# One tensor for the last stage's expert weights, lent to the first two stages, and the expert loads moved from SyncE at the last stage's start to ScalarE in and behind the last batch

## The reference: what is computed

```
x = x + tanh(g_xattn[0]) * L0_xattn(layernorm(x), ctx, mask0)      # 16 heads of 16
x = x + tanh(g_ffn[0])   * L0_ffn(layernorm(x))                    # 8 experts, top 2
x = x + tanh(g_xattn[1]) * L1_xattn(ctx, layernorm(x), mask1)      # 16 heads of 64, keys: 375 + 112
x = x + tanh(g_ffn[1])   * L1_ffn(layernorm(x))                    # 8 experts, top 2

def L1_ffn(x, W1, b1, W2, b2, Wr, br):       # W1: 8 x 256 x 1024, W2: 8 x 512 x 256
    logits = xf @ Wr + br
    topk_val, topk_idx = top_k(logits, 2); scores = softmax(topk_val)
    h = einsum('nd,edh->enh', xf, W1) + b1;  a, g = split(h, 2)
    out_e = einsum('enh,ehd->end', silu(a) * g, W2) + b2
    return sum of the two chosen experts' outputs, weighted by scores
```

## Time and profile before

| | |
|---|---|
| median of three runs | 1396.94 us (1396.32 to 1399.18) |
| the profiled execution | 1397.87 us, its span 1396.1 us |
| granted TensorE clock, mean | 0.944 of full speed |
| PE, VectorE, ScalarE, GpSimd busy | 88%, 77%, 71%, 58% of the span |
| first stage ends, last stage begins | about 449 us, 1186 us |
| DMA | 185.50 MB, mean 133 GB/s |

### The profile page before, as it was taken

The page is one execution under the profiler, slowest core; times in us unless marked ns, Lnnn a source line. Parts: engine busy times, 40 slices in busy tenths (PEclk is TensorE's granted clock), DMA queues, the critical chain, the costliest instruction groups (busy, mean ns, idle before and its releaser), DMA issues. The chain is left out here.

```text
span 1396.1 us, 38073 instructions
## 1 busy us (share of the span) xinstructions
PE 1224.2 (88%) x13060; PEld 878.1 (63%) x13060; DVE 1080.9 (77%) x3112; ACT 996.9 (71%) x2552; POOL 813.6 (58%) x1204
## 2 busy tenths in 40 slices
PE   5899999999985599999999999999999974489994
PEld 3677777777763245666656666656666653388994
DVE  4899999999984268888888888888888882477772
ACT  4888888888873368888787888787888771256662
POOL 3545445455423445777777777777777674146564
PEclk8899999999997699999999999999999985699998
DMA  6546455344310149777688877888777693853323
GB/s 185 149 135 176 121 158 165 110 136 144 105 51 21 42 97 164 152 141 152 140 158 163 157 141 149 139 159 162 157 136 153 139 197 58 323 150 57 61 36 76
DMA packets 309406, 185.50 MB, mean 133 GB/s; under 512 B 257930, under 2 KB 295186, under 8 KB 306112
## 3 DMA queue, kind: packets, MB, share of 16 engines
q1 hardware_dynamic: 293024, 140.82, 46.8%
q0 software_dynamic: 13168, 35.80, 10.4%
q10 hardware_dynamic: 3024, 6.47, 1.6%
HBM read 76.19 MB, written 49.94 MB: 90 GB/s over the span
## 5 line engine op out<-in xcount | busy, mean ns | idle before, releaser
L1685 ACT ACTIVATE b_prob<-b_prob,b_top 112x487 f32<-112x487 f32 x256 | 178.8, 698 | 28.6 <-DVE b_top L1811 26.9
L1318 POOL TENSOR_TENSOR b_halves<-b_prob,b_halves 112x487 f16<-112x487 f32 x128 | 146.8, 1147 | 80.6 <-ACT b_halves L1710 79.2
L1496 PE MATMUL b_ps_p<-w_s,b_tok_s 128*128 128x512 f16 (+1 forms) x768 | 187.7, 381 | 4.0 <-DVE b_k_s L1798 3.2
L1496 PE MATMUL b_ps_p<-b_tok_s,w_s 128*128 128x487 f16 x768 | 183.1, 376 | 6.4 <-POOL b_tok_s L1312 3.7
L1811 DVE CUSTOM_DVE_ANT_0 b_prob<-b_ps_s,b_keep 112x487 f32<-112x487 f32 x256 | 167.4, 655 | 13.6 <-PE b_ps_s L1589 12.0
L721 ACT ACTIVATE a_prob<-a_prob,a_top 112x375 f32<-112x375 f32 x256 | 155.0, 606 | 5.4 <-DVE a_top L856 2.3
L1710 ACT ACTIVATE b_halves<-b_prob 112x487 f16<-112x487 f32 x256 | 155.9, 609 | 0.4
L856 DVE CUSTOM_DVE_ANT_0 a_prob<-a_ps_s,a_keep 112x375 f32<-112x375 f32 x256 | 138.2, 540 | 14.8 <-PE a_ps_s L614 14.6
L622 PE MATMUL a_ps_t<-a_const,a_prob 112*125 112x112 f32 x768 | 134.2, 284 | 12.7 <-ACT a_prob L721 10.4
L861 DVE TENSOR_TENSOR a_pT<-a_ps_t,a_pT 125x336 f16<-125x336 f32 x256 | 128.2, 501 | 20.5 <-ACT a_pT L728 19.5
L1604 PEld LDWEIGHTS b_ps_o<-b_v_s,b_pT 128*128 128x128 f16 (+1 forms) x3072 | 123.7, 99 | 31.9 <-DMA b_pT<-b_halves 12.0
(11 more groups left out here) (263 smaller groups left out, 3016.8 us busy)
## 6 DMA issues: line engine op xcount, KB each, us to landing
xs<-a_blank SPq DMA_DIRECT2D x14, 1032.0 KB, 4.2
c_w_pool<-w_split SPq DMA_DIRECT2D x8, 1600.0 KB, 10.1
b_wch_f<-in_w_experts POOLq DMA_DIRECT2D x32, 384.0 KB, 5.1
w_split<-b_wch_s POOLq DMA_DIRECT2D x32, 384.0 KB, 3.4
a_k_stack<-keys SPq DMA_DIRECT2D x96, 93.8 KB, 3.2
a_ctx_f<-in_ctxT SPq DMA_DIRECT2D x16, 375.0 KB, 3.9
keys<-a_k_s SPq DMA_DIRECT2D x16, 375.0 KB, 3.2
b_ctx_t<-in_ctx SPq DMA_DIRECT2D x16, 375.0 KB
```

The lines of the kernel that those rows point to most:

```text
L1318: pool.tensor_tensor(halves[:, h % TURN, LO, 0:NK], prob[:, h % RING, 0:NK], halves[:, h % TURN, HI, 0:NK], ALU.subtract).then_inc(s_lo[1], 1)
L1496: last = pe.matmul(out, sta(a, k), mov(m, k), start=(k == 0 and n == 0), stop=(k == tiles - 1 and n == 2))
L1685: act.activation(prob[:, h % RING, 0:NK], prob[:, h % RING, 0:NK], ACT.Exp, bias=top[:, h % RING:h % RING + 1], scale=-1.0, accum_out=sums ...
```

## The change

`w_pool`, 128 x 8 x 6400 fp16, is allocated in `build_program` for the whole kernel, with the eight semaphores `s_w`. The first two stages take a part of their buffers out of it (`room` cuts pieces off one after another). In the second stage the first piece is `k_s` and `v_s` of even batches (15,984 of the 51,200 columns), so the places of experts 0 and 1 (columns 0 to 12,799) are free once batch 14's values are done; the other six lie over buffers that batch 15 still uses. ScalarE now issues all eight loads: experts 0 and 1 in slots 7 and 9 of batch 15, the other six behind the last batch, between `hitem` 1 and `hitem` 3 of the tail. SyncE's list in the last stage keeps the tile loads, with one `announce` behind each of the first eight.

```
+def room(tensor):
+
+    flat = tensor[:, :, :].rearrange("p e n -> p (e n)")
+    taken = [0]
+
+    def take(shape, dt):
+        n = math.prod(shape[1:]) * (2 if dt == F32 else 1)
+        part = flat[0:shape[0], taken[0]:taken[0] + n]
+        taken[0] += n
...
-        k_s = [sb(f"k_s{i}", [128, 2, IT, NK], F16) for i in range(2)]
-        v_s = [sb(f"v_s{i}", [128, 2, NB1, INNER], F16) for i in range(2)]
+
+        k_s, v_s = zip(*((take([128, 2, IT, NK], F16), take([128, 2, NB1, INNER], F16)) for i in range(2)))
...
-        halves = sb("halves", [T, TURN, 2, NB1 * KB1], F16)
-        pT = sb("pT", [128, TURN, 2, NB1, 128], F16)
+        halves = take([T, TURN, 2, NB1 * KB1], F16)
+        pT = take([128, TURN, 2, NB1, 128], F16)
+        tok_f = take([128, KT, NK], F32)
+        order = take([T, T], F32)
+        x2_n = take([T, D], F32)
...
+            def load_expert(e):
+
+                need(act, s_pv, H, B - 2 if e < 2 else B - 1, H)
+                if e >= 2:
+                    for j in range(2):
+                        act.wait_ge(s_wchstore[j], 16 * B)
+                act.dma_start(w_pool[:, e, :], w_dram[e]).then_inc(s_w[e], 16)
+
             def body(b, par):
                 for s in range(H):
+                    if not ahead(b, 1) and s in (7, 9):
+                        load_expert((s - 7) // 2)
...
             for k in range(HI_):
                 hitem(B - 1, k)
+                if k == H_O - 1:
+                    for e in range(2, E):
+                        load_expert(e)
             weigh(B - 1)
...
-            def load_expert(e):
-                sp.dma_start(w_pool[:, e, :], w_dram[e]).then_inc(s_w[e], 16)
-
-            load_expert(0)
             for i in range(TILES):
-                if i == 4:
-                    announce(0)
-                    load_expert(1)
-                elif i == 8:
-                    announce(1)
-                    load_expert(2)
-                    load_expert(3)
-                elif i == XT:
-                    for e in range(4, E):
-                        load_expert(e)
-                    announce(2)
-                if XT <= i < XT + E - AHEAD - 1:
-                    announce(i - XT + AHEAD + 1)
                 load(i)
+                if i < E:
+                    announce(i)
```

More of the change, by code:

```diff
@@ L12 @@
+import math
 from contextlib import ExitStack
@@ L63 @@
 BLANK = 128 * 8
+def room(tensor):
[5 more added lines that the diff above has]
+        taken[0] += n
+        part = part.bitcast(F32) if dt == F32 else part
+        axes = "abcde"[:len(shape) - 1]
+        sizes = dict(zip(axes[1:], shape[2:]))
+        return part.rearrange("p (" + " ".join(axes) + ") -> p " + " ".join(axes), **sizes) if len(axes) > 1 else part
+    return take
 def need(eng, sem, per, batch, count, met=None):
@@ L109, in phase_attention_small_heads @@
         sem = lambda name: ctx.enter_context(nc.semaphore("a_" + name))
+        take = room(w_pool)
         bank = lambda name: ctx.enter_context(nc.psum_tensor("a_" + name, [128, 512], F32))
@@ L121, in phase_attention_small_heads @@
         WE = E * D // (H // 2)
-        next_f = sb("next_f", [128, next_w_dram.shape[1]], F32)
+        next_f = take([128, next_w_dram.shape[1]], F32)
         we_f = next_f[:, 0:KT * E * D].rearrange("p (k n) -> p k n", k=KT)
@@ L137, in phase_attention_small_heads @@
         tanhs = sb("tanhs", [128, 4], F32)
-        blank = sb("blank", [BLANK // 8, 8 * ROW], F32)
+        blank = take([BLANK // 8, 8 * ROW], F32)
         x_in = sb("x_in", [T, D], F32)
@@ L1936, with phase_experts @@
 TABLE_COUNT, TABLE_ROW = 4, 18
-def phase_experts(nc, w_dram, xs_dram, acc_dram, ones, cum, s_rows, head, s_head, ident, s_ident, b1_f, out):
+def phase_experts(nc, w_dram, xs_dram, acc_dram, ones, cum, s_rows, head, s_head, ident, s_ident, b1_f, w_pool, s_w, out):
     with ExitStack() as ctx:
@@ L1992, in phase_experts @@
         s_valid = sem("valid")
-        s_w = [sem(f"w{e}") for e in range(E)]
         s_x = [sem(f"x{i}") for i in range(XSEM)]
@@ L2297, in build_program @@
         s_rows = ctx.enter_context(nc.semaphore("rows"))
+        w_pool = ctx.enter_context(nc.sbuf_tensor("w_pool", [128, E, SW], F16))
+        s_w = [ctx.enter_context(nc.semaphore(f"w{e}")) for e in range(E)]
         with nc.sbuf_tensor("w1_s", [128, 2, WKV + WQ + WOUT], F16) as w1_s:
```

28 lines of the change are left out of this document (12 added, 16 removed).

## The result

The changed kernel took 1411.05 us (1409.78 to 1414.55, four runs), the kernel before on the same chip 1398.06 us (1396.32 to 1400.06, four runs): ratio 1.0099, 95% interval 1.0078 to 1.0121. It is slower by 13 us, or 1.0%, where the forecast was 14 us faster. The profiled execution took 1410.86 us, its span 1409.1 us, against 1397.87 and 1396.1 before.

What follows compares the result with a forecast made beforehand. Taken to bound the kernel: PE's last-stage stalls beside expert loads, and the chain of scatters. Gains of 21.0 less costs of 6.0 and 1.0 made 14.0 us, so 1382.9 us against the median 1396.94; 8-in-10 range 1376.5 to 1389.5.

Steps and rivals of the forecast that it cites:

- (e): Cost of loading experts 0 and 1 during batch 15, beside its DMA transposes: 6.0 us, bounds 0 and 15.4.
- slower: Rival for batch 15: transposes stop while a load is in flight, and that load stretches; about 1399 us, chance 0.03.
- (f): Cost of the six loads behind batch 15, beside the store and the scatters into `xs`: 1.0 us, bounds 0 and 5.
- the reason I gave against it: A last-stage scatter beside loads took 11.0 us, landing 1.4 us before the last load: looked like waiting for the end.
- (a): Last stage: PE's stall before the first product, a wait for an expert's transfer, is gone; gain 12.4 us.
- (b): Last stage: without the stall PE's clock stays up instead of at half speed; gain 1.4 us, bounds 0 and 2.15.
- (c): Last stage: the first scatter, with no expert load in flight, lands in 3.8 us and not 11.0; gain 7.2 us.
- (d): SyncE's list loses eight load instructions and gets an expert wait before each of tile loads 1 to 8; costs nothing.
- (g): Buffers in another place, with first-stage buffers in `w_pool`; costed at 0.

Runs made afterwards that it cites:

- e4: The changed kernel with only expert 0 loaded in batch 15 (ScalarE, slot 7) and the other seven behind the batch: 1389.26 us.
- e9: The changed kernel with both loads of batch 15 issued by ScalarE back to back in slot 7: 1390.94 us.
- f1: The changed kernel with ScalarE's second load of batch 15 one slot earlier, in slot 8 instead of 9: 1390.47 us.
- e7: The changed kernel with both loads of batch 15 issued by GpSimd back to back in slot 5: 1391.22 us.
- e12: The same kernel as e3 (all eight loads behind batch 15), run again on another chip: 1384.9 us, ratio 0.9905.
- e3: The changed kernel with no load in batch 15 and all eight behind it, buffers still in `w_pool`: 1384.01 us, ratio 0.9882.
- e1: The changed kernel with both loads of batch 15 issued by GpSimd, in slots 5 and 7, instead of ScalarE: 1389.15 us.
- e8: The changed kernel with no load in batch 15, four behind it and four as ScalarE's first instructions of the last stage: 1388.15 us, ratio 0.9937.
- e11: As e8, but the last four loads come behind ScalarE's `spread_x(1)`, SyncE's waits for them behind tile loads 8 to 11: 1384.51 us, ratio 0.9898.

## Why the prediction was wrong

**Failed: (e), the two loads in batch 15.** Priced at 6.0 us with an upper bound of 15.4, measured 29.1. The working shared out bandwidth: 8.0 us of transfer, 1.9 us of it free. That was wrong already for a single load: the same working gives 4.0 - 1.9 = 2.1 us, and e4 measured 8.0, about the load's landing. For two loads that are close together the 6.0 looks nearly right (7.5 to 9.3 us in e9, f1 and e7), but only because the second cost nearly nothing there, so that is luck. The bound supposed that each load lands in its own 7.7 us and that transposes at worst stand still for both. But the second load itself slowed down to 32.4 us, SyncE was held for 8.9 and 20.3 us in the issue of two transposes, and DMA counted as wholly busy moved 60 to 118 GB/s. A bound made of two undisturbed landings didn't hold a case in which the loads are stretched too. That case stood there as the rival "slower", with 22.5 us and a chance of 0.03; it was what happened, with 29.1. Its argument against, that the transpose beside `head` landed in 8.5 us, was a row with one load.

**Mis-sized: (f), the six loads behind the batch.** Priced 1.0, bounds 0 and 5, measured 4.3. The issues were hidden as forecast (3.38 us of issue inside 9.24 us of idle time). The store, which the working let land in 8.9 us, landed in 7.9 and held up nothing. The loss was the scatter's. The working let it land at 1193.7 and counted only the 1.4 us by which that passes the first tile load at 1192.28. The step that failed is this slack: the whole last stage starts 0.9 us behind the scatter's landing, so that all 4.3 us by which it landed later (6.9 in e12 against 2.6 before) moved the stage.

Neither small transfer waited for the end of the loads: the last of the six landed 24.8 us behind its issue, at 1222.1, the store at 1209.5 and the scatter's last packet before 1218.5. That agrees with the rule of the Trainium skill's "DMA: Bandwidth & Descriptors" (queues, rings and completion order) that a DMA engine takes packets in turn, and not with the reason I gave against it. But the result that I drew from the rule, (f) = 0, was further off than my 1.0: the store still took 7.9 us against 1.8 before, and the scatter 4.3 us more than before.

**Right: (a), (b), (c).** Forecast 21.0 us: 13.8 before the first scatter and 7.2 behind it. Measured 13.1 and 7.2, so 20.3. The 0.7 us between them I didn't separate. PE's wait for the low half came out at 2.3 us, a little over the 2 that I gave; it is the smaller of the two that stood there before (6.5 - 4.0 = 2.5). **(d)** cost nothing that is seen, and **(g)** is 0: e3 has the same buffers in the same place and ends batch 15 0.1 us from before.

The sum with measured terms: 20.3 - 29.1 - 4.3 = -13.1. Of the 27.0 us by which the profiled execution missed its forecast (1410.9 against 1383.9), 23.1 are (e), 3.3 (f), 0.7 the gains.

**What stays open.** Why a second load 3.5 to 6.1 us behind the first stops transposes and load together. The runs take away the number of DMAs, the scatters and one queue as the sole place. They take away the shared tensor only for a batch without loads (e3): every second load went into `w_pool`, beside the transposes' buffers, and none into a tensor of its own, so that could have a part. They leave long rows and the moment, be it the distance from the first load or the place in SyncE's held issue. e1 (6.4 us apart, both on GpSimd, no stop) isn't explained for certain: it could be its queue, that its first load had nearly landed, or that SyncE's issue was ending. Loads with long rows at several distances from SyncE's transposes alone, without the batch, would tell this; that wasn't tried.

## What to carry to other kernels

Don't price a big load beside DMA transposes by its share of the bandwidth: put it where no engine waits for a transpose, here behind the last batch, even if it then starts later (0.988 to 0.991 of the time before, against 1.010). There too look for the last small transfer ahead of a barrier: a scatter that lands 4.3 us later beside the loads moved everything behind it by as much. If it must go beside them, cut its rows or issue the loads directly one behind the other, and measure at the very slots that are to be used, since one slot more or less was worth 20 us (f1 against the change). And if a rival that says "they stop" has only a row with one load against it, give it more than 3 in 100.

## What the runs showed of the hardware

- One 1600 KB load beside a run of DMA transposes within SBUF delayed the batch by 8.0 us, two by 7.5 to 13.1, and in the near stop two by 17.6 to 29.1, with the second load landing in 20.6 to 32.4 us instead of some 10.
- In the near stop 57 load packets took 1.9 us each, and 60 to 118 GB/s counted as full occupation; six loads without transposes moved 427 to 429 GB/s at 0.43 us a packet.
- The issue of a DMA transpose on SyncE, 2.4 us at most in e3, took 8.9 and 20.3 us in the near stop of the change, and everything behind it in SyncE's list waited.
- Rows of 3.2 KB instead of 12.8 KB removed the near stop (+8.2 against +29.1 us at the same slots); 32 partitions at a time instead of 128 didn't (+24.9).
- The last stage starts 0.85 to 0.99 us behind the landing of the last indirect DMA ahead of the barrier (thirteen traces). That landing took 2.6 to 3.1 us without expert loads in flight (before, e8, e11) and 6.8 to 7.0 beside them.
